# Context batches 1 to 3 loaded into the space of the dense weights, a new instruction order, and rotary position turning by a lane shuffle

## The reference

```python
# 1 cross attention without softmax; H=16 heads of 16, then a layer norm and the residual
score = einsum('bhqd,bhkd->bhqk', Q, K) / dk          # Q from layernorm(x), K and V from the context
ctx   = einsum('bhqk,bhkd->bhqd', where(mask, -inf, score), V)
x     = x + layernorm(residual + linear(ctx, wo))
# 2 two self attentions per tile, both with causal softmax; the second has compressed keys and
#   values (Wk_c, Wv_c, then Wk, Wv) and rotary position turning of queries and keys
# 3 mixture of experts: a dense shared part and, of 8 experts in 2 groups, the two best, weighted
h = swiglu(x @ W1_shared);  y = shared(x) + sum_e w8[e] * (h @ W2_experts[e])
```

## Time and profile before

| | us |
|---|---|
| median of 3 runs | 241.22 |
| lowest, highest | 241.12, 241.95 |
| span of the profiled execution | 239.0 |
| PE busy in it | 228.0 |
| DVE busy | 171.9 |
| ACT busy | 121.4 |
| POOL busy | 75.3 |

### The profile page before, as it was taken

The page is one execution under the profiler, slowest core; times in us unless marked ns, Lnnn a source line. Parts: engine busy times, 40 slices in busy tenths (PEclk is TensorE's granted clock), DMA queues, the critical chain, the costliest instruction groups (busy, mean ns, idle before and its releaser), DMA issues.

```text
span 239.0 us, 5721 instructions
## 1 busy us (share of the span) xinstructions
PE 228.0 (95%) x2304; PEld 205.4 (86%) x2304; DVE 171.9 (72%) x370; ACT 121.4 (51%) x245; POOL 75.3 (32%) x89
## 2 busy tenths in 40 slices
PE   6989899999999999999999999999999999999991
PEld 6987797999999889978989999988878879998881
DVE  0757876966987879887966789586697764448353
ACT  3754575238571766386177977815451553550000
POOL 3011026222634020513549567745110020731011
PEclk9999999999999999999999999999999999999998
DMA  6899999828153452023304511100000000000001
GB/s 221 265 298 394 353 357 320 300 85 268 75 175 102 106 174 71 21 69 109 88 4 118 170 70 32 58 1 3 0 3 0 3 0 3 0 22 3 3 0 66
DMA packets 9434, 26.35 MB, mean 110 GB/s; under 512 B 1464, under 2 KB 2752, under 8 KB 9280
## 3 DMA queue, kind: packets, MB, share of 16 engines
q1 hardware_dynamic: 9120, 25.47, 32.4%
q10 hardware_dynamic: 288, 0.52, 0.6%
HBM read 25.46 MB, written 0.52 MB: 109 GB/s over the span
## 4 chain that ended last, share of the span: by engine, by line
PE 83%; DMA 7%; issue 3%; ACT 3%; DVE 2%; SPq 1%; POOLq 0%; POOL 0%; DVEq 0%
PE ps L704 77%; DMA raw<-in_ctx 7%; PE ps L707 5%; ACT ch L578 1%; DVE cl L1143 1%; ACT probT L511 1%; SPq L403 0%; DVE Z L1304 0%; SPq L358 0%; POOLq L363 0%; POOL rstd L463 0%; ACT z0T L511 0%; DVE X L1313 0%; DVE mb L1184 0%; DVE xHL L1273 0%
## 5 line engine op out<-in xcount | busy, mean ns | idle before, releaser
L704 PE MATMUL ps<-ch 128*128 128x130 f32 (+1 forms) x208 | 51.4, 264 | 1.5 <-DVE cl L1143 1.4
L704 PE MATMUL ps<-ch,cl 128*128 128x260 f32 (+1 forms) x208 | 51.1, 308 | 0.0
L704 PE MATMUL ps<-w,hT 128*128 128x512 f32 (+1 forms) x204 | 45.9, 382 | 0.0
L704 PEld LDWEIGHTS ps<-w,hT 128*128 128x128 f32 x204 | 36.4, 188 | 7.7 <-issue 0.7
L1143 DVE TENSOR_TENSOR cl<-raw,ch 128x1024 fp32r<-128x1024 f32 (+4 forms) x31 | 31.9, 1051 | 14.9 <-ACT ch L578 14.7
L704 PEld LDWEIGHTS ps<-ch 128*128 128x128 f32 (+1 forms) x208 | 39.5, 190 | 2.9 <-issue 1.4
L704 PEld LDWEIGHTS ps<-ch,cl 128*128 128x128 f32 (+1 forms) x208 | 39.2, 188 | 0.2
L463 POOL TENSOR_TENSOR rstd<-ve,half_exp 128x1 f32<-128x1 f32 (+1 forms) x22 | 13.8, 628 | 73.0 <-DVE ve L1022 72.9
L578 ACT ACTIVATE ch<-raw 128x1024 fp32r<-128x1024 f32 (+4 forms) x31 | 27.5, 916 | 12.9 <-DMA raw<-in_ctx 10.8
L704 PE MATMUL ps<-xHL,dense 128*128 128x256 f32 x192 | 24.3, 285 | 0.0
L704 PEld LDWEIGHTS ps<-xHL,dense 128*128 128x128 f32 x192 | 23.4, 192 | 0.2
(11 more groups left out here) (161 smaller groups left out, 417.7 us busy)
## 6 DMA issues: line engine op xcount, KB each, us to landing
raw<-in_ctx SPq DMA_DIRECT2D x22, 512.0 KB, 4.6
raw<-in_w SPq DMA_DIRECT2D x8, 512.0 KB, 3.8
stage<-in_dense SPq DMA_DIRECT2D x4, 512.0 KB, 5.9
w<-in_w SPq DMA_DIRECT2D x4, 256.0 KB, 6.9
w<-in_w SPq DMA_DIRECT2D x1, 1024.0 KB, 8.4
mask<-in_mask SPq DMA_DIRECT2D x1, 800.5 KB, 7.5
raw<-in_ctx SPq DMA_DIRECT2D x8, 65.0 KB
raw<-in_ctx ACTq DMA_DIRECT2D x2, 256.0 KB, 4.7
```

The lines of the kernel that those rows point to most:

```text
L704: return pe.matmul(o, l, r, start=start, stop=stop, skip_group_check=not check)
```

## The change

1. **Load room.** A tensor `ahead` for three whole batches is laid over the space of `dense`, which stands empty until `piece` 0. Batches 1 to 3 land there without SP waiting for anything; batch 3 comes in one transfer of 1536 KB and a tail. Chunks of batch 4 and later go to `raw` as before. `piece` 0 waits on ACT until the split of batch 3 is done. The other inputs are issued at other chunks.
2. **Lane shuffle.** `rotate` and its permutation constant are gone, the keys are projected once, and the value product is issued within `keys2` (6 matmul instructions in place of 2 + 8 + 2). DVE then shuffles queries and keys together (128 x 512 from PSUM, neighbouring partitions exchanged), multiplies the unshuffled ones by the cosine, the shuffled ones by the sine, and adds. ACT's copy into `qs` and POOL's multiplication are gone.
3. **Narrow pieces.** The products with two columns move from `cross2_product` to `cross3` and are cut into 32 instructions of 32 weight columns; `svn` and POOL's scaling move with them to `cross3`. `gates` is cut in the same way, 32 instructions for 8.
4. **Order.** `gram`, `cross2_product`, `hidden_product` and `experts_product` are each divided into two steps between which others can stand, with the same matmuls, and the list of steps is a new one.

```diff
+    ahead, nxt = place("ahead", [P, AHEAD, CH_B * ROWS + 1, D], at=where["dense"])
...
-                5: [(X[:, :, :], d_x, "x_in"), (w0[:, 2, :, :], d_w0[:, 2, :, :], "wv_in"), (cols[:, :], d_cols, "cols_in"),
+                5: [(w0[:, 2, :, :], d_w0[:, 2, :, :], "wv_in"), (cols[:, :], d_cols, "bias_in"),
+                    (rows[:, 3, :], d_rows[3, :].partition_broadcast(P), "bias_in"), (X[:, :, :], d_x, "x_in"),
+                    (w0[:, 0, :, :], d_w0[:, 0, :, :], "wqk_in")],
...
-                if b:
-                    sp.wait_ge(sem("low_done"), splits(n - CH_B))
+                if b > AHEAD:
+                    sp.wait_ge(sem("low_done"), splits(c if b == AHEAD + 1 else n - CH_B))
...
+                elif b == AHEAD and c == 0:
+                    sp.dma_start(raw_batch(b)[:, 0:CH_B * ROWS, :], src).then_inc(sem("ahead_batch"), 16)
...
+            pool.memset(ahead[:, :, CH_B * ROWS, :], 0.0).then_inc(sem("no_rows"), 1)
...
+                    if i == 0:
+                        act.wait_ge(sem("low_done"), splits(CH_B * (AHEAD + 1) - 1))
...
+                            for r in range(P // PAIR):
+                                mine = slice(r * PAIR, (r + 1) * PAIR)
+                                last = mm(ps[mine, tile_bank(1) + 1, t * 16:t * 16 + GRP + E],
+                                          xT[:, k, t * P + r * PAIR:t * P + (r + 1) * PAIR], gate[:, k, :], k == 0, k == KC - 1)
...
-                elif step == "rotate":
-                    pe.wait_ge(own("qs", i), i // 2 + 1)
-                    mm(ps[:, tile_bank(i) + 1, 0:D], const("rot"), qs[i % 2][:, :, :].rearrange("p c n -> p (c n)"),
-                       True, True).then_inc(own("rot", i), 1)
...
+                    for ob in range(KC):
+                        last = mm(ps[:, tile_bank(i), ob * P:(ob + 1) * P], wkv[0:P // 2, ob * P:(ob + 1) * P],
+                                  kvcT[i % 2][0:P // 2, :], True, True)
+                        if ob == 0:
+                            mm(ps[:, tile_bank(i) + 1, D:2 * D], kvcT[i % 2][P // 2:P, :], wkv[P // 2:P, :], True, True)
...
+                    link(dve.stream_shuffle(turned.rearrange("p b c n -> p b (c n)"), both, SWAP))
+                    dve.tensor_tensor(summed, both.rearrange("p b (c n) -> p b c n", n=S),
+                                      const("cos").unsqueeze(1).unsqueeze(1).to_broadcast(wide), ALU.mult).then_inc(own("qk_taken", i), 1)
+                    link(dve.tensor_tensor(turned, turned, const("sin").unsqueeze(1).unsqueeze(1).to_broadcast(wide), ALU.mult))
+                    dve.tensor_tensor(summed, summed, turned, ALU.add).then_inc(own("roped", i), 1)
...
```

The opening of the new list, with the places that the steps below speak of:

```diff
+        ("split", 0), ("gram_rows", 0), ("gram", 0), ("split", 1), ("gram_rows", 1), ("split", 2), ("gram", 1),
+        ("split", 3), ("evac", 0), ("split", 4), ("gram_rows", 2), ("gram", 2), ("gram_rows", 3), ("cross1", 0),
+        ("gram", 3), ("split", 5), ("gram_rows", 4), ("gram", 4), ("norm0", 0), ("norm0", 1), ("norm0_end", 0),
+        ("norm0_end", 1), ("cross2", 0), ("cross2_half", 0), ("cross2_product", 0), ("gram_rows", 5), ("split", 6),
+        ("gram", 5), ("pre", 0), ("pre", 1), ("evac", 1), ("split", 7), ("cross3", 0), ("q0_product", 0),
+        ("q0_product", 1), ("cross1", 1), ("flag", 0), ("cross4", 0), ("split", 8), ("qb", 0), ("cross2_half", 1),
+        ("cross2_product", 1), ("flags", 0), ("cross2", 1), ("gram_rows", 6), ("gram", 6), ("cross3", 1),
+        ("gram_rows", 7), ("gram", 7), ("gram_rows", 8), ("masked", 0), ("cross4", 1), ("gram", 8), ("split", 9),
...
```

More of the change, by code:

```diff
@@ L74, in constants @@
     return c
+SWAP = [lane ^ 1 for lane in range(32)]
 NU = 5 + 8
@@ L90, in opening_steps @@
     return [
[L91 to L97, removed]
+        ("split", 0), ("gram_rows", 0), ("gram", 0), ("split", 1), ("gram_rows", 1), ("split", 2), ("gram", 1),
[6 more added lines that the diff above has]
+        ("gram_rows", 7), ("gram", 7), ("gram_rows", 8), ("masked", 0), ("cross4", 1), ("gram", 8), ("split", 9),
+        ("xo_product", 0), ("evac", 2), ("split", 10), ("qb", 1), ("cross1", 2), ("xo", 0), ("split", 11),
+        ("xo_end", 0), ("norm1", 0), ("gram_rows", 9), ("gram", 9),
     ]
@@ L103, in first_half_steps @@
     return [
[L104 to L111, removed]
+        ("gram_rows", 10), ("cross2", 2), ("norm1_end", 0), ("split", 12), ("split", 13), ("cross2_half", 2),
+        ("cross2_product", 2), ("gram", 10), ("gram_rows", 11), ("gram", 11), ("turn_z", (0, 0)), ("evac", 3),
[3 rows of a table added]
+        ("shares", (0, 0)), ("gram_rows", 13), ("gram", 13), ("gram_rows", 14), ("gram", 14), ("exp", (0, 0)),
+        ("split", 15), ("cross3", 3), ("split", 16), ("evac", 4), ("turn_p", (0, 0)), ("cross4", 3), ("cross1", 4),
+        ("values", (0, 0)), ("xo_product", 1), ("xo", 1), ("project", (0, 0)), ("gram_rows", 15), ("gram", 15),
+        ("gram_rows", 16), ("gram", 16), ("xo_end", 1),
     ]
@@ L117, in second_half_steps @@
     return [
[L118 to L131, removed]
[3 rows of a table removed]
-        ("values1", 2), ("turn_x", 1), ("cross4", 7), ("piece", 8), ("score_product", (2, 0)), ("score", (2, 0)),
@@ new lines, in second_half_steps @@
+        ("keys_roped", 0), ("cross3", 4), ("shares", (1, 0)), ("evac", 5), ("score_product", (0, 1)), ("exp", (1, 0)),
+        ("gram_rows", 18), ("gram", 18), ("split", 20), ("gram_rows", 19), ("gram", 19), ("turn_p", (1, 0)),
+        ("cross4", 4), ("score", (0, 1)), ("values", (1, 0)), ("cross1", 5), ("project", (1, 0)), ("norm2", 1),
+        ("split", 21), ("norm2_end", 1), ("shares", (0, 1)), ("split", 22), ("cross2", 5), ("gram_rows", 20),
+        ("gram", 20), ("exp", (0, 1)), ("cross2_half", 5), ("turn_z", (1, 1)), ("cross2_product", 5),
@@ new lines, in second_half_steps @@
+        ("proj2_product", 1), ("turn_p", (0, 1)), ("keys2", 1), ("evac", 6), ("values", (0, 1)), ("project", (0, 1)),
+        ("cross3", 5), ("gram_rows", 21), ("rms1", 0), ("split", 23), ("rms1_end", 0), ("square", 0),
+        ("keys_roped", 1), ("cross4", 5), ("values2", 1), ("gram", 21), ("cross1", 6), ("turn_x", 0),
+        ("score_product", (1, 1)), ("gram_rows", 22), ("piece", 4), ("xo_product", 2), ("gram", 22),
+        ("gram_rows", 23), ("gram", 23), ("exp", (1, 1)), ("score", (1, 1)), ("cross2_half", 6),
[5 rows of a table added]
@@ L481, in _ @@
                     last.then_inc(sem("gpre"), 1)
-                elif step == "cross2" and i % 2:
+                elif step == "cross3" and i % 2:
                     t = i // 2
@@ L739, in project @@
                                   rows_[k], k == 0, k == KC - 1)
[L740 removed]
+                if signal is not None:
+                    last.then_inc(signal, 1)
             pe.wait_ge(sem("blank"), 1)
@@ L791, in _ @@
                         pe.wait_ge(sem("mb"), i)
+                    if i > 1 and i % 2 == 0:
+                        pe.wait_ge(sem("svn"), i // 2)
                     bank = ps[:, CROSS_B[0], :]
```

332 lines of the change are left out of this document (164 added, 168 removed), and 11 rows, old and new, of the table USES.

## The result

The changed kernel takes 246.96 us (median of 5, 246.49 to 248.09) against 241.22 us: 1.0235 times as long (95% interval 1.0208 to 1.0263). The forecast was 230.7 us with a range up to 235.2; the time lies 16.3 us above the one and outside the other. The profiled execution has a span of 246.3 us for 239.0; it is the longest of the five, the others have 244.7 to 245.6.

A forecast was written before the change was run, and what follows sets the result against it. PE was taken as the bound, busy 228.0 of 239.0 us. Less 7.5 us of matmuls and 3.0 of waits gives a 228.5 us span, plus 2.2 to the median 230.7; own range 228 to 233, wider range 227.5 to 235.2.

The forecast's parts named there:

- Matmuls removed: On PE: rotation 2.3, keys 1.9, two-column products 2.2 and gates 1.1 us saved, 7.5 us in sum.
- The price of the shuffle: DVE's lane shuffle on 512 columns in `keys2`: taken at 0.69 us, bounds 0.69 and 3.8.
- Loads and opening: Up to 42.4 us: loads land before their users, `cross1` starts at 13.7 instead of 15.58; 2.0 us won.
- No idle time of ACT for loads behind chunk 2: Opening: a sign that the forecast is right, ACT no longer standing idle for loads after chunk 2.
- Behind 42.4: Waits after the opening: 1 us more won than lost up to tile 2's output product, nothing counted from 131 on.
- No wait foreseen is longer than today's: Whole kernel: no foreseen wait exceeds today's, so nothing was counted for the granted clock.
- The rival of the held DVE: `keys2`: POOL's weight pieces hold eight DVE operations 1.5 us each, 12 us lost, 242.7 us; chance 0.05.
- The row of 1.91 us: Kernel before: one DVE addition took 1.91 us beside a POOL operation, its like 0.42; read as 1.5 us lost.
- today's additions keep to 0.42: Argument against the slower rival: the old rotation's additions also have two SBUF inputs, yet keep to 0.42 us.
- The rival of the full DVE queue: DVE at 89% becomes the bound, its fixed-order queue giving back the 3.0 us and 1 more: 234.7 us; chance 0.17.

The follow-up runs named there:

- The quarters: Changed kernel with each POOL subtraction of a weight piece issued as four of 256 columns: 242.75 us (1.0063).
- taking 7 us off DVE: Changed kernel without shuffle, sine product and sum behind the keys: 248.39 us (1.0229); the same with low parts zeroed by memset: 239.26 us (0.9863).
- the memset: Changed kernel with the low parts of the weight pieces zeroed by a POOL memset in place of the subtraction: 238.32 us (0.9894).
- its control: Kernel before the change, with the low parts of the weight pieces likewise zeroed by a POOL memset: 241.29 us (0.9996).
- the new start, the old second half and the old rotation: Changed kernel with second half and closing in the order of before, and the old rotation in place of the shuffle: 239.27 and 239.82 us.
- the version with the changed tail: Changed kernel with the old second half's order up to tile 3's turned scores, then its own list again: 240.37 us (0.9956).
- the run with both exchanges: New start and old second half, steps exchanged around tile 1's keys, plus the changed kernel's tail from tile 3's turned scores: 247.42 us (1.0208).

## Why the prediction was wrong

*Matmuls removed*: right, in size too. The 32 narrow instructions take 0.27 us in `cross3` (0.26 taken) and 0.37 in `gates` (0.26 taken), and the 7.5 us are 9.7 in the account above, of which about 1.2 belong to the booking (changed kernel, `cross3` of batch 7):

```profile
126.84 0.43 PE L735 MATMUL ps<-scol,w 128*32 128x2 f32 x32
127.11 0.46 PE L735 MATMUL ps<-cv,w 128*32 128x32 f32 x32
```

*The price of the shuffle*: right. It was taken at 0.69 us (bounds 0.69 to 3.8) and measures 0.73 in the median of four; the four operations behind the keys take 0.69 to 0.74.

```profile
L1286 DVE STREAM_SHUFFLE swapped<-ps x4: 728/737/746, 81.0 to 181.5; 128x512 f32<-128x512 f32 x4
```

*Loads and opening*: right in the main. `cross1` starts at 13.69 (13.7 foretold), `cross4` of batch 1 at 36.09 (36.6), and `xo_product` of tile 0 finds PE idle for 0.85 us until `ctxT` is there (up to 1). "No idle time of ACT for loads behind chunk 2" was wrong: it waits 2.66 us at 18.55, and no wait of PE follows from it. By the account the opening won 1.1 us and not 2.0, since the wait for `ctxT`, which the forecast booked behind 42.4, lies ahead of it.

*Behind 42.4* is the step that failed. "I find 1 us more won than lost" measured 7.1 us lost up to 131, and "from 131 on there is no idle time to win, and I count nothing" measured 10.2 us lost. The replay moved PE, DVE and ACT on with undisturbed lengths, and stopped at tile 2. It had none of POOL's pieces in it, and behind 131 it looked only for waits to win and never for waits that a new list brings. "No wait foreseen is longer than today's" rested on the same replay, and with it the clock counted at nothing; behind the gaps of 1.72 and 1.83 us at 142 to 146 stand the 2.9 us of matmuls at the lower level.

*The rival of the held DVE* had the mechanism, at the wrong place and at 0.05. I looked for it at the two operations of `keys2`, where one of four sine products was held (1.78 us for 0.68). The other six struck operations that the change does not touch: shares, a split, `ctxT`, a normalisation, the gates. The row of 1.91 us beside a long POOL operation, which ended 0.29 us after that operation, was read as a price of the new operations. It is the price of a DVE operation with two SBUF inputs (in the normalisation the second is one number per partition) wherever the list sets it beside such a POOL operation; in the trace of the changed kernel it fell on seven. The argument against it ("today's additions keep to 0.42") was no argument, since it came from the old places. The Trainium skill (SBUF — State Buffer, section SBUF: two separate sides) has the rule for that, the exclusive port pair that whoever starts first keeps for the whole instruction. The quarters agree with it: the wait fell from 2.0 to 0.4 us with the length of one POOL instruction.

*The rival of the full DVE queue* (234.7) named the wrong cause: taking 7 us off DVE changed nothing.

The account: of the 16.3 us, POOL's pieces in the new list are 8.6, shown by the memset against its control; the 2.9 us at the lower clock are among them. The work came out 2.2 us better by the booking. What is left, about 10 us of waits more than forecast, stands in 17 gaps of 0.3 to 1.5 us in the run with the memset (before: 11 gaps, 6.0 us; there 10.5) and in many smaller ones. Neither the table loads nor DVE's share nor the chain behind the keys makes it. The four longest idle times of PE in that run behind 30 us end with ACT's `zT` (1.41 us, tile 2's second projection), DVE's `Z` (0.92, tile 0's last turn), DVE's `ctxT` (0.85, tile 0's output product) and ACT's `qp` (0.61, tile 3's values). Why each of these queues is late stays open.

The complete version that beats both kernels by most is the one with the new start, the old second half and the old rotation, 239.27 and 239.82 us in two runs: 0.6 to 0.9% below before. The part of the change that the forecast priced highest by the matmuls, the rotation (4.2 us), is not in it. With the shuffle, the version with the changed tail reaches 240.37 us, 0.4% below before, with an interval that ends just short of no change (0.9995). The old rotation with that tail was not run.

## What to carry to other kernels

When a change brings a new order, price the order like an operation: lay every long POOL instruction against the DVE operations that start while it runs, and see what PE has to wait for behind each. A gap in DVE's total load is no protection, and a hold-up that costs nothing in one order can cost its full length in another; splitting the long instruction helps where the other engine waits and costs where its own result is late. Work saved on the bounding engine is only won where the list can cover the longer chain that replaces it.

## What was not expected of the hardware

DVE operations on 2 to 8 columns are held as long as wide ones (2.40 us for 0.28), and POOL is held in turn: a scaling of 0.62 us takes 1.85 beside a split on DVE. A POOL memset, which reads nothing, still held the normalisation (1.01 us for 0.41), while beside it the shares and `ctxT`, with two SBUF inputs, kept their length (1.22 and 0.43 us). Beside the subtractions, additions with one input in PSUM went by undisturbed.

In six of the nineteen profiles the first matmuls run at half pace: in the five of them that have half chunks the first two take 1.87 and 1.73 us for 1.14 and 1.09, with 0.22 us a matmul in place of 0.12, while the granted clock of the stretch is given as 1.00. The first 3 us behind 5.0, first in the changed kernel, then in the run with both exchanges (columns as above):

```profile
5.00:8.00 3.00, 2.26 (x16) 1.91 (x16) 2.15 (x6) 2.38 (x6) 0.00 (x0) 1.00 1.00 378
```

```profile
5.00:8.00 3.00, 2.41 (x11) 2.24 (x11) 2.38 (x6) 2.52 (x7) 0.00 (x0) 1.00 1.03 399
```

Sixteen matmuls there, eleven here. The 1.00 is not a reading: a trace's record of the granted clock does not begin with the span, and a stretch without a record is given as 1.00. The record begins at 5.8 us in the first of these traces and at 10.2 in the second. In all six with the slow start it begins at 9.5 to 10.6 us, and there the pace doubles; in the thirteen others it begins at 4.0 to 5.9. So the half pace fits the lower level of the clock. What decides how long it lasts no run shows. In two profiles of one kernel, the one with the old rotation, batch 1's `cross1` starts at 28.04 and 26.63 us; so it is worth 1.4 us, and it can stand in the scatter of the medians above.
